# Last cross-attention block of a Perceiver layer: preparations in the blocks in front, probability sums on all rows of their heads, output product's first part behind the last scores

## The reference, cut to what matters

```python
x = x + xattn(layernorm(x), ctx_2048, mask, Wq, bq, Wk, bk, Wv, bv, Wo, bo, gamma, beta, residual_scale)
x = x + attn(layernorm(x), w_qa, q_a_ln_w, w_qb, w_kva, kv_a_ln_w, w_kvb, w_o)
x = x + ffn(layernorm(x), gate_weight, gate_up_proj, down_proj, old_to_new)

def xattn(hs, at, mask, ...):                      # H 512, 16 heads of 32, S 256, T 4096
    q, k, v = hs @ Wq.T + bq, at @ Wk.T + bk, at @ Wv.T + bv
    scores = clip(where(mask, q k^T / sqrt(32), -10000), -50, 50)
    probs = softmax(scores)
    delta = clip(residual_scale, 0, 0.3) * ((probs v) @ Wo.T + bo)
    return layernorm(delta) * gamma + beta
```

## Time and profile before

| | |
|---|---|
| median of 3 runs | 725.61 us (725.24 to 727.03) |
| the profiled execution: own time, span | 726.88 us, 725.1 us |
| busy: PE, PEld, DVE, ACT, POOL | 706.8, 459.3, 609.8, 435.3, 11.4 us |
| granted TensorE clock, mean | 0.995 |
| chain that ended last, by engine | PE 90%, DVE 3%, ACT 3%, DMA 2% |
| cross-attention blocks 1 to 5, each | some 34.9 us |
| block 6, block 7 with its tail up to the last weigh | 36.2 us, 31.0 us |
| self-attention and experts | from about 322 us on |

### The profile page before, as it was taken

How to read it: one execution, slowest core, us unless ns; L and a number is a source line. 1 busy time by engine, 2 the same in 40 slices (tenths; PEclk the granted TensorE clock), 3 DMA queues, 4 the chain that set the end, 5 groups by cost and what they waited for, 6 DMA issues and landing times.

```text
span 725.1 us, 20521 instructions
## 1 busy us (share of the span) xinstructions
PE 706.8 (97%) x8732; PEld 459.3 (63%) x8732; DVE 609.8 (84%) x942; ACT 435.3 (60%) x597; POOL 11.4 (2%) x36
## 2 busy tenths in 40 slices
PE   8999999999999998888999989999999999999998
PEld 3555555555555554446777757777777777777775
DVE  4768999999999998876879976888888888888885
ACT  5677787877878787724768753444444444444442
POOL 3000000000000000001000000000000000000000
PEclk9999999999999999999999999999999999999999
DMA  8560101010100100022242502677777777777770
GB/s 319 180 263 3 60 3 61 4 61 7 57 4 2 49 15 3 3 104 119 77 153 92 201 20 73 199 220 244 228 238 242 230 232 245 224 238 240 221 249 33
DMA packets 29880, 94.44 MB, mean 130 GB/s; under 512 B 5824, under 2 KB 15088, under 8 KB 28400
## 3 DMA queue, kind: packets, MB, share of 16 engines
q1 hardware_dynamic: 28944, 92.31, 38.4%
q10 hardware_dynamic: 864, 1.07, 0.5%
HBM read 92.76 MB, written 0.57 MB: 129 GB/s over the span
## 4 chain that ended last, share of the span: by engine, by line
PE 90%; DVE 3%; ACT 3%; DMA 2%; issue 1%; SPq 0%; POOL 0%; ACTq 0%; DVEq 0%
PE pS L1184 39%; PE pP L1184 29%; PE pO L1184 13%; PE pD L1184 9%; DMA arena<-in_wkT 1%; DMA mask_i<-in_mask 1%; ACT arena L540 1%; PE pO L1569 1%; DVE arena L781 0%; DVE arena L899 0%; DVE xn L1102 0%; ACT arena L593 0%; SPq L312 0%; ACT arena L578 0%; PE pS L1403 0%
## 5 line engine op out<-in xcount | busy, mean ns | idle before, releaser
L1184 PE MATMUL pS<-arena 128*128 128x256 f16 (+3 forms) x2185 | 254.2, 272 | 1.9 <-ACT arena L578 0.8
L1184 PEld LDWEIGHTS pS<-arena 128*128 128x128 f16 (+1 forms) x2185 | 213.6, 101 | 46.1 <-issue 2.1
L1184 PE MATMUL pP<-arena 128*32 128x512 f16 (+1 forms) x2996 | 239.8, 380 | 0.4 <-ACT arena L460 0.4
L1184 PEld LDWEIGHTS pP<-arena 128*32 128x32 f16 (+1 forms) x2996 | 109.1, 97 | 101.3 <-ACT arena L460 1.3
L540 ACT ACTIVATE arena<-pS,mblk 128x1024 f32<-128x1024 f32 x128 | 147.3, 1206 | 8.7 <-PE pS L1184 8.7
L1013 DVE SCALAR_TENSOR_TENSOR arena<-arena 128x1536 f16<-128x1536 f32 x72 | 126.1, 1752 | 0.8 <-ACT arena L654 0.8
L694 ACT ACTIVATE arena<-pS 128x256 f32<-128x256 f32 x72 | 27.6, 384 | 154.1 <-PE pS L1184 154.1
L1184 PE MATMUL pO<-arena 128*32 128x256 f32 (+7 forms) x1370 | 108.7, 359 | 1.9 <-DVE arena L1008 1.9
L654 ACT ACTIVATE arena<-arena 128x1536 f16<-128x1536 f32 x72 | 106.4, 1477 | 1.0 <-PE pP L1184 1.0
L867 DVE TENSOR_SCALAR arena<-arena 128x1024 f32<-128x1024 f32 x128 | 86.1, 689 | 14.9 <-ACT arena L540 14.9
L1184 PE MATMUL pD<-arena 128*128 128x512 f16 x288 | 77.8, 379 | 0.0
(11 more groups left out here) (252 smaller groups left out, 496.0 us busy)
## 6 DMA issues: line engine op xcount, KB each, us to landing
arena<-in_units SPq DMA_DIRECT2D x72, 768.0 KB, 4.9
arena<-w_scratch SPq DMA_DIRECT2D x136, 64.0 KB, 2.7
arena<-in_ctxT SPq DMA_DIRECT2D x7, 1024.0 KB, 5.2
mw_in<-in_mla_in SPq DMA_DIRECT2D x8, 832.0 KB, 6.6
mw_out<-in_mla_out SPq DMA_DIRECT2D x8, 512.0 KB, 3.6
wlatT<-in_wlatT SPq DMA_DIRECT2D x1, 1280.0 KB, 10.7
arena<-in_ctxT ACTq DMA_DIRECT2D x4, 256.0 KB, 5.9
arena<-in_wkT SPq DMA_DIRECT2D x4, 256.0 KB, 5.6
```

The costliest lines, as they stand in the source:

```text
L1184: return pe.matmul(o, lhsT, rhs, start=start, stop=stop, **kw)
```

## The change

- The f16 halves of the latent weights move from block 7 to blocks 1 to 4, one part in each behind pair 0, on ACT (high) and DVE (`low_weights`). The addition of beta to x moves to block 0, pair 6, and block 5, pair 0 (`prep_rows`). The output bias' halves move to block 6: pair 0 on ACT, pair 6 on DVE (`low_bias`); the scales to block 6, pair 7 on DVE (`prep_scales`). The tiles of the halves lie elsewhere for that.
- The folding matmuls use `ones[:, 0:32]` instead of `onecol[:, g, :]`: each of the 32 rows of a band gets the sum of its head. Groups 0 and 2 are folded in `pD`, 1 and 3 in `pP`. `add_sums` for group 0 stays in block 6, pair 3; those for groups 1, 2, 3 stand in block 7, pairs 1, 4, 6.
- DVE inverts a group in two halves of 128 columns, in the pairs 2 to 7 (`max_sums`, `invert`), straight into `rden`. The spreading matmuls and ACT's copies of them are gone. The multiplication stays on DVE (`weighted`), the value bias goes to ACT (`add_bias`).
- The output product's first part (bias row and group 0) stands behind pair 7; group 1 behind the last weigh; groups 3 and 2 by halves of the rows; of the second half everything stands behind the first half. The load of `woT` stands on SP's queue in front of block 6's mask load.

```diff
-                    for w_at in (rd_end, 6144))
+                    for w_at in (wl_at, wl2_at))
@@ SP
-            x_block(NBLK - 2, 0, load=False)
-
             sp.wait_ge(s["ctx_lo"], 4 * (NBLK - 1))
             sp.dma_start(woT, a["woT"]).then_inc(s["wo_in"], 16)
+            x_block(NBLK - 2, 0, load=False)
@@ ACT
+                    if 1 <= b <= HC and i == 0:
+                        if b == 1:
                             act.wait_ge(s["lat_in"], 16)
-                        act.activation(wlh[:, i], wlatT[:, i], ACT.Copy, scale=SW).then_inc(s["wl_hi"], 1)
+                        act.activation(wlh[:, b - 1], wlatT[:, b - 1], ACT.Copy, scale=SW).then_inc(s["wl_hi"], 1)
+                    if b == NBLK - 2 and i == 0:
+                        high_bias()
+            def last_block(b, p):
+                evac(b, p, 7)
+                for i in range(PAIRS_X):
+                    act.wait_ge(s["scores_done"], PAIRS_X * b + i + 1)
...
+                    if i < 2:
+                        act.wait_ge(s["pv_done"], PAIRS_X * b - 1 + i)
+                    else:
+                        act.wait_ge(s["last_pv"], i - 1)
...
+                    if i == 6:
+                        for g in range(2):
+                            add_bias(g + 1, g, slice(0, T))
+            def add_bias(k, g, cols):
+                act.wait_ge(s["ctx_mul"], k)
+                act.activation(ctxn[:, g, cols], ctxn[:, g, cols], ACT.Identity, bias=xb[:, 2, g:g + 1])\
+                   .then_inc(s["ctxn_ready"], 1)
...
             for t in range(TT):
-                act.wait_ge(s["denb_done"], t + 3)
-                act.activation(rden[:, 3, 128 * t:128 * t + 128], pS[:, t, 0:128], ACT.Copy).then_inc(s["rden_ready"], 1)
+                for k, g in ((3, 3), (4, 2)):
+                    add_bias(k + 2 * t, g, slice(128 * t, 128 * t + 128))
@@ DVE
+            def max_sums(g):
+                if g:
+                    dve.wait_ge(s["inverted"], g)
+                dve.tensor_scalar(den[:, :], (pD, pP)[g % 2][:, 0:T], 1e-30, None, ALU.max).then_inc(s["den_read"], 1)
+            def invert(g, t):
+                cols = slice(128 * t, 128 * t + 128)
+                dve.wait_ge(s["den_read"], g + 1)
+                half = dve.reciprocal(rden[:, g, cols], den[:, cols])
...
+                    if 1 <= b <= HC and i == 0:
+                        low_weights(b - 1)
+                    if b in (0, NBLK - 3) and i == 6 * (b == 0):
+                        prep_rows(0 if b == 0 else 1)
+                    if b == NBLK - 2 and i == 6:
+                        low_bias()
+                    if b == NBLK - 2 and i == 7:
+                        prep_scales()
+            def last_block(b):
...
+                    if g and i % 2 == 0:
+                        dve.wait_ge(s["last_pv"], 2 * g)
+                        max_sums(g - 1)
+                    if g:
+                        invert(g - 1, i % 2)
+                    if i == 5:
+                        for h in range(2):
+                            dve.wait_ge(s["inverted"], h + 1)
+                            weighted(h, slice(0, T))
@@ DVE, behind the last pair
-            link(dve.tensor_scalar(den, pD[:, 0:T], 1e-30, None, ALU.max))
...
-            last_den(0)
-            dve.wait_ge(s["pv_done"], PAIRS_X * NBLK)
-            context((2,), slice(0, T), 2)
-            context((3,), slice(0, 128), 3)
-            last_den(1)
-            context((3,), slice(128, T), 4)
+            for t in range(TT):
                 cols = slice(128 * t, 128 * t + 128)
...
+                dve.tensor_scalar(den[:, cols], pP[:, cols], 1e-30, None, ALU.max).then_inc(s["den_read"], 1)
...
+                link(dve.reciprocal(rden[:, 3, cols], den[:, cols]))
+                if t == 0:
+                    dve.wait_ge(s["last_pv"], PAIRS_X)
+                for g in (3, 2):
+                    weighted(g, cols)
@@ PE
+            def sum_rows(g, tiles, start=False, stop=False):
+                for j in range(4):
+                    last = mm((pD, pP)[g % 2][32 * j:32 * j + 32, 0:T], ones[:, 0:32], tiles[:, j, :], start, stop,
+                              skip_group_check=True)
+                return last
+            def last_block(b, p):
...
+                for i in range(PAIRS_X):
+                    scores(b, p, i)
+                    if i == 0:
+                        weigh(b - 1, 1 - p, PAIRS_X - 1)
+                        pe.wait_ge(s["proj_evac"], 8 * NBLK)
+                    else:
+                        averaged(i - 1)
+                        summed(i - 1).then_inc(s["last_pv"], 1)
+                    if i in (1, 4, 6):
+                        add_sums(b - 1, (1, 4, 6).index(i) + 1)
+                pe.wait_ge(s["wo_in"], 16)
+                pe.wait_ge(s["ctxn_ready"], 1)
+                out_rows(0, (0,))
+                summed(PAIRS_X - 1).then_inc(s["rows_done"], 1)
+                averaged(PAIRS_X - 1).then_inc(s["last_pv"], 1)
@@ PE, in a block before the last
-                    if i % 2 and i > 1 and not last and flushed(b, i // 2 - 1):
-                        add_sums(b, i // 2 - 1)
+                    if b == NBLK - 2 and i == 3:
+                        add_sums(b, 0)
@@ PE, behind the last pair
+            out_rows(0, (1,))
+            for t in range(TT):
+                if t:
+                    pe.wait_ge(s["den_read"], HC + 1)
+                    out_rows(t, (0, 1))
+                pe.wait_ge(s["ctxn_ready"], 2 * t + 3)
+                out_rows(t, (3,))
+                pe.wait_ge(s["ctxn_ready"], 2 * t + 4)
+                out_rows(t, (2,)).then_inc(s["delta_done"], 1)
```

More of the change, by code:

```diff
@@ L1373, in _ @@
+                    project(b + 1, 1 - p, i)
             pe.wait_ge(s["q_lo"], 1)
[L1374 removed]
+            for b in range(NBLK - 1):
                 x_block(b, b % 2)
[L1376 to L1381 removed]
```

237 lines of the change are left out of this document (94 added, 143 removed).

## The result

The changed kernel takes 721.57 us (median of 8 runs, 720.32 to 723.11), the kernel before 725.25 in the runs beside it (8 runs, 724.93 to 727.03): a ratio of 0.9947, 95% interval 0.9936 to 0.9958. The forecast was 722.0.

A forecast was written before the change was run, and what follows sets the result against it. The prediction took PE to bound the blocks in front, DVE close behind, and a ring of waits block 7. Its terms, 0.86 + 0.10 + 1.28 + 0.20 + 1.25 - 0.10 = 3.6 us, took 725.61 to 722.0 us; range 720.7 to 723.9.

The forecast's parts named there:

- A, sums out of block 6: Block 6: two of three foldings of sums leave PE's work and fit into block 7's steps, a gain of 0.86 us.
- B, start of block 7: Pairs 0 to 2: absent ACT preparations gain 0.86 us, a new PE wait for DVE's clips eats 0.75; 0.10 us left.
- rival 1: Start of block 7: DVE's clips come in time, the gain there is 0.86 us, total 721.2 us; chance 0.15.
- C, pairs 5 and 6: Block 7: spreads and first output product leave the ring, two longer steps become 3.25 us each, a gain of 1.28 us.
- the ring: Block 7: scores, two exponentials from the same banks, next scores, each waiting for ACT's exponentials; 3.25 us a pair undisturbed.
- D, last pair to sums: Last scores to last sums: loses one spread and trades one product for bias row and product, a gain of 0.2 us.
- E, sums to turn: Last sums to PE's turn: the second half's order goes, statistics at 4.1 us, turn at 7.6, a gain of 1.25 us.
- F, the blocks in front: Blocks before block 7: moved preparations add to DVE's lag and cost 0.1 us, bounds 0 and 1.3.
- the limit of 1.25 us: Blocks in front: how much DVE's clips may lag before PE's averages wait; worst point expected at 1.3 to 1.4 us.
- a slower kernel: DVE has no room, 5.8 us of moved work lands on the blocks' path: 1.3 us slower, 726.9 us; chance 0.05.
- an unshortened ring: Block 7 keeps 3.9 us steps because PE or DVE has too much in a pair; 723.3 us, chance 0.06.

The follow-up runs named there:

- e2: Kernel before, with only the folding of groups 1 and 2 moved from block 6 to behind pairs 2 and 3 of block 7: 724.12 us.
- e1: Changed kernel with DVE's scales and low output-bias half moved from block 6 to behind the clips of pairs 0 and 1 of block 7: 719.55 us.
- e15: e4 with the output product's first part (bias row and group 0) put back in pair 6 of block 7: 721.17 us.
- e7: Changed kernel with all preparations (weight halves, rows, bias halves, scales) put back into block 7: 721.35 us.
- e12: Changed kernel with both halves of a group's inverse in one pair (2, 4 and 6) instead of one in each of two pairs: 720.85 us.
- e10: Changed kernel with the output product's first part behind the last averages instead of behind the last scores: 721.63 us.
- e4: Changed kernel with the value bias added on DVE (VectorE) instead of ACT (ScalarE): 722.07 us.
- e3: Changed kernel with each low weight half of blocks 1 to 4 made twice on DVE: 725.67 us.
- e5: e1 with one more matmul of zeros ahead of each wait for a part of the query weight's low half in the start-up: 719.43 us.
- e14: e1 with the output product's first part between the sums of the last pair's first tile and those of its second: 719.81 us.
- e11: Kernel before, with one more matmul of zeros ahead of each wait for a part of the query weight's low half in the start-up: 723.9 us.

## Why the prediction came out right

- **A, sums out of block 6:** 0.86 forecast, 0.87 measured, and 0.87 alone in e2.
- **B, start of block 7:** 0.10 forecast, -0.05 measured. The step that failed is the scores of pair 1, which I had 3.24 behind those of pair 0; they came 3.33 behind: PE took them 0.14 behind the end of ScalarE's exponentials (281.40 to 283.70), where before it was 0.05, in every kernel with the new block 7, and no run shows why. The wait itself was as worked out: pair 1 to 2 took 4.07 (I had 4.0), by PE's wait for DVE. e1 gave the 0.8 back that the wait took, so rival 1's price was right, and its condition (DVE out of block 6 earlier) was not met.
- **C, pairs 5 and 6:** 1.28 forecast, 1.29 measured. e15 shows the product's part of it: before's step of 3.81 is PE's own row with the product in it, 0.57 over the ring. e7 and e12 show that neither the absent preparations nor the halved inverses have a share. The other 0.72, in pair 5, lies in before's spreading matmuls, for which PE waited until DVE's inverse was done:

```profile
302.94 1.10 PE L1184 MATMUL pP<-arena,selrow 128*128 128x256 f32 x4 [0.24 <-DVE arena L899]
```

They hold PE for 0.24 of waiting and 1.03 up to the next scores (303.97), less the 0.55 that PE idles in an undisturbed step: 0.72. That is a sum from rows; the spreads were not tried alone.
- **D, last pair to sums:** 0.2 forecast, 0.31 measured, between its bounds. The product that stands in front of the sums costs 0.26 of the way in the changed kernel (e10 and e15: 4.69 without it); before had one of like length there. What is left is a trade on PE, which has no idle time there in either kernel: the spread of group 2 took 0.54 (310.41 to 310.95 in before), and the bias row that came in takes 0.23 (306.75 to 306.98 in after), which is the 0.31. I had the spread at 0.11 to 0.4. It was not tried alone.
- **E, sums to turn:** 1.25 forecast, 1.30 measured: statistics 4.12 behind (4.1), turn 7.56 behind (7.6), with PE busy up to it. The product started 2.09 behind the sums, 0.05 earlier than I had it (2.04 for the bias and 0.1 in front); the two bias additions took 0.69 together, against the 2 x 0.37 I had. The product's place behind the last scores is worth 0.2 of D and E together (e10). The rest I laid to the second half's order and the missing copies. Before's rows bear that out:

```profile
315.17 2.20 PE L1184 MATMUL pO<-arena 128*128 128x512 f32 x4
...
317.94 0.29 DVE L851 TENSOR_TENSOR arena<-pO,arena 128x128 f32<-128x128 f32 x1 [0.89 <-ACT arena L574]
```

PE was through with the first half's product at 317.37, and its statistics came 1.10 later (318.47), because DVE did the second half's multiplication first, for which it waited 0.89 for ScalarE's copy. After has 0.05 there. This order was not tried alone either.
- **The rule on ScalarE** (the Trainium skill, "ScalarE: Activation LUTs", Rules for kernel authors: additions on VectorE). I said that following it would cost 0.7. e4 shows 0.08 between first scores and turn, and nothing in the time. What failed is the length of DVE's queue and the price: I put the queue at 3.8 without the additions and these at 1.0, but in after DVE is through 3.5 behind the sums (312.09 + 0.49) and then idles 0.61, and the four additions took 0.8, so there was room for nearly all of them. The trace neither supports the rule here nor speaks against it.
- **F, the blocks in front:** -0.1 forecast, 0 measured: blocks 0 to 5 take 208.98 us in after and 208.99 in before. e3 shows that the limit of 1.25 us is real and that twice the added work crosses it from block 2 on. What I had wrong is how near the change comes to it. I reckoned the clips of pair 1 of block 5 as 1.3 to 1.4 later than the usual 2.94 behind their scores. They are 3.44 behind (218.16 - 214.72), 0.5 later, and 0.8 of the room is left: a block adds 0.03 to 0.05, and the two stalls of 0.47 do not come: DVE shows no idle time in blocks 1 to 5. The limit is touched elsewhere, in the last pair of block 6, where the bias half makes the clips 4.22 late (280.37 - 276.15) and the averages still lose only 0.02 (1.09 us instead of 1.07).

The sum was 3.6 and the measured stretch 3.73. The rivals of a slower kernel and of an unshortened ring are out by the same rows. That the sum is so near is in part luck: B came 0.15 below its forecast and D, E and F together 0.26 above. But one thing I did not see, although the numbers were there: term B being near 0 means that moving the preparations was worth nothing as written (e7), with all of term F's risk on its side. I priced DVE's load per pair against 3.25 as if an overrun lands on the path, while PE's 0.55 of idle time per step was in the earlier trace rows. Best of all is the change with the preparations behind the clips (e1, 719.55 us; with the zeros of e5, 719.43, which the runs don't tell apart).

## What to carry to other kernels

In a ring of waits an engine that overruns one step costs nothing while its result still comes before the taker gets to it; read that distance (here 1.2 us for a clip) and the taker's own idle time (0.55 us a step) before paying for less load. What does count is what stands directly in front of the first result of a stretch: two preparations of 1.4 us, which cost nothing behind the first clips, cost 0.8 us ahead of them. Work that another engine's wait already covers is best kept exactly in that wait, and a later or "finer" place for it can be worse (e10, e14).

## What the runs showed of the hardware

TensorE's granted clock falls to 0.50, its 1.2 GHz level, for a few microseconds in some executions and not in others of the same program. The windows of before, two in the start-up and four around the first turn (busy us and count per engine, then the clock, the DMA share and GB/s):

```profile
22.00:24.00 2.00, 1.68 (x9) 1.12 (x9) 2.00 (x4) 0.45 (x1) 0.00 (x0) 0.67 0.06 1
24.00:26.00 2.00, 2.00 (x12) 1.41 (x10) 2.00 (x5) 0.00 (x0) 0.00 (x0) 0.50 0.53 183
...
320.00:322.00 2.00, 0.27 (x2) 0.10 (x2) 1.84 (x6) 0.00 (x0) 0.27 (x1) 1.00 0.33 49
322.00:324.00 2.00, 1.22 (x11) 1.01 (x12) 1.86 (x5) 1.21 (x3) 0.55 (x1) 0.76 0.96 393
324.00:326.00 2.00, 2.00 (x9) 0.90 (x7) 1.78 (x7) 0.00 (x0) 0.07 (x1) 0.50 1.04 430
326.00:328.00 2.00, 2.00 (x15) 1.24 (x14) 0.00 (x0) 0.35 (x1) 0.48 (x1) 0.89 0.99 415
```

In after's profile all windows are at 1.00. In both places PE had just been idle: in the start-up in gaps of 0.32 to 0.5 us, behind the last block for 1.73. After has like gaps in its start-up (0.32 and 0.39) and no fall. The same stretch of the start-up's projection in after, and in e11, at the full clock:

```profile
22.60 3.34 PE L1218 MATMUL pS<-xT,arena 128*128 128x256 f16 x29 [0.32 <-DVE arena L790]
```

```profile
22.43 3.34 PE L1184 MATMUL pS<-xT,arena 128*128 128x256 f16 x29
```

In before the same 29 matmuls take from 22.48 to 27.48, 5.0 us. The times of each kernel lie on levels by the mean clock of the execution. Of before, 70 runs beside the experiments: 23 at 1.000 near 723.6 us, 32 at 0.998 near 725.2, 15 at 0.995 near 727.0. Of after (8 runs): 720.4, 721.6 and 723.1. Level by level the change is worth 3.2 to 3.9 us, around the 3.73 of the stretch; the scatter of the first scores among profiles at 1.000, 35.8 to 36.3, is as large as the rest. Of the 6.4 between the two profiles, 3.4 lie between before's own levels of 0.995 and 1.000.

Whether the gaps cause it was tried with e5 and e11. In their 18 runs none is at 0.995, where 34 of the 153 others are (before and all variants); by chance that would come out so about once in 90 times. But e1 and e2, which have no zeros, have none in 16 runs either (once in 56), and e5, built on e1, has the same four runs of six at 1.000 as e1: it shows nothing by itself. Nor did e11 do what I expected of it. I had said that the later stretch would stay as often as before; in the three profiles at 0.998 (e2, e5, e11) the later stretch is the only one, and e11 has 3 of 12 runs on that level and none below, where before has 47 of 70 on the two lower levels. So e11's median, 1.3 us below before's, comes from fewer runs with a slow stretch of either kind, though the zeros fill only the first gaps. That filling the gaps keeps the first stretch away is likely and not shown.

The later stretch falls at different places, and each time behind a long wait of PE. In before, e2 and e11 it is the 1.73 us in front of the turn. In after that wait is gone, since PE is busy with the product up to the turn. The three profiles with the new tail that have a later stretch (e3, e4, e5) have it at 334 to 346, behind the next long wait, of 1.9 to 2.0 us for DVE. In e5, and the same matmuls in after, at the full clock:

```profile
334.08 3.92 PE L1218 MATMUL pO<-arena 128*128 128x128 f16 x36 [1.99 <-DVE arena L1042]
```

```profile
334.56 2.35 PE L1218 MATMUL pO<-arena 128*128 128x128 f16 x36 [1.91 <-DVE arena L1042]
```

So the change seems to move the stretch rather than to remove it: at 1.000 are about as many of the runs of one tail (30 of 79) as of the other (36 of 92). The wait alone doesn't bring it about, as seven profiles with the new tail have the same wait and no stretch. In which execution it comes stays open. The Trainium skill, "TensorE: Matmul & The Clock Gate", Part 1, ties the gate to how busy the engine has lately been, and calls the slow stretch at a kernel's start variable from run to run. Both agree with these rows (falls behind waits of 1.73 to 1.99 us; levels of 723.6, 725.2 and 727.0 for one program), which show the variation in the middle of a kernel too.
